# Cross-attention and routed FFN on one core: the tail's steps in another order, and single banks for the last tiles

## What is computed

```python
x = x + attention(layernorm(x), ctx, ctx)        # 16 heads of 16, softmax over 1024 keys, W_O and b_O
n = layernorm(x)
shared = (silu(n @ sw1) * (n @ sw3)) @ sw2       # 256 -> 512 -> 256
s = sigmoid(n @ router_w.T)                      # 8 experts
top2 = top_k(s + router_bias, 2)                 # gates: s of the two, divided by their sum
routed = sum over top2 of gate * (gelu(n @ ew1[e]) @ ew2[e])
out = x + shared + routed
```

## Time and profile before

| | us |
|---|---|
| median of 3 runs | 354.72 |
| lowest, highest | 354.29, 355.25 |
| profiled execution | 355.46 |
| its span | 353.7 |
| TensorE busy in it | 318.8 |
| VectorE, ScalarE, GpSimd busy | 263.1, 220.2, 146.4 |
| mean granted clock of TensorE | 0.973 of full |

### The profile page before, as it was taken

One profiled execution on the slowest core, in us unless ns is written; L12 is line 12 of the kernel. 1 busy time (PEld: TensorE's weight loads), 2 busy tenths in 40 slices (PEclk: granted clock), 3 DMA queues, 4 the chain that ended last, 5 costly groups with the idle time before them and its releaser, 6 DMA issues.

```text
span 353.7 us, 6968 instructions
## 1 busy us (share of the span) xinstructions
PE 318.8 (90%) x2556; PEld 190.0 (54%) x2556; DVE 263.1 (74%) x439; ACT 220.2 (62%) x395; POOL 146.4 (41%) x204
## 2 busy tenths in 40 slices
PE   5787898999999999999999999999999797899970
PEld 2585565333333333333373354344899785799870
DVE  5886998999999999999939941894966735743525
ACT  5562445898989899898928874855134442656410
POOL 6014469104045252566544554375110265335540
PEclk9999999999999999999999995999999899999996
DMA  7679892026061340816349323002401023802635
GB/s 253 276 259 348 288 369 102 0 56 194 5 210 36 108 142 21 260 32 189 120 128 274 98 63 124 6 15 91 135 5 59 32 80 103 281 32 76 213 116 178
DMA packets 29130, 47.54 MB, mean 134 GB/s; under 512 B 6388, under 2 KB 20596, under 8 KB 27412
## 3 DMA queue, kind: packets, MB, share of 16 engines
q1 hardware_dynamic: 27128, 41.70, 37.0%
q0 software_dynamic: 1968, 5.38, 4.2%
HBM read 28.34 MB, written 16.01 MB: 125 GB/s over the span
## 4 chain that ended last, share of the span: by engine, by line
PE 64%; DVE 16%; DMA 6%; ACT 5%; issue 5%; SPq 2%; another core or an unknown queue 1%; POOL 1%; POOLq 0%; ACTq 0%; DVEq 0%
PE psum L1228 20%; PE psum L1415 18%; PE psum L1282 14%; PE psum L1288 8%; DVE negm L1117 4%; DMA PB<-in_ctxT_dram 2%; ACT PB L767 2%; DMA PB<-ys_d 1%; PE psum L1346 1%; PE psum L1325 1%; SPq L435 1%; DMA qs_d<-SWH 1%; ACT TMP L823 1%; DMA EWT<-qs_d 1%
## 5 line engine op out<-in xcount | busy, mean ns | idle before, releaser
L1117 DVE TENSOR_REDUCE negm<-psum 128x1 f32<-128x1024 f32 x128 | 153.7, 1222 | 12.4 <-PE psum L1288 11.9
L767 ACT ACTIVATE PB<-psum 128x512 f32<-128x512 f32 x256 | 138.4, 598 | 32.2 <-PE psum L1282 23.6
L1415 PE MATMUL psum<-PB,VA 128*17 128x256 f32 x1024 | 81.5, 392 | 2.6 <-ACT TMP L823 2.1
L1228 PE MATMUL psum<-EWT,WH 128*128 (+2 forms) x348 | 55.8, 310 | 4.3 <-ACT TMP L802 2.4
L1282 PE MATMUL psum<-EWT 64*128 64x512 f32 x160 | 58.6, 448 | 0.4 <-ACT PB L767 0.3
L1288 PE MATMUL psum<-EWT 64*128 64x512 f32 x160 | 53.5, 450 | 4.4 <-DMA EWT<-qs_d 2.5
L1228 PEld LDWEIGHTS psum<-EWT,WH 128*128 128x128 f32 x348 | 47.3, 195 | 8.5 <-issue 6.8
L1415 PEld LDWEIGHTS psum<-PB,VA 128*17 128x17 f32 x1024 | 17.5, 95 | 46.7 <-issue 35.6
L1282 PEld LDWEIGHTS psum<-EWT 64*128 64x128 f32 x160 | 24.5, 184 | 30.7 <-ACT PB L767 24.1
L1288 PE MATMUL psum<-S 64*128 64x512 f32 x96 | 32.2, 457 | 1.7 <-DVE negm L1117 1.2
L1282 PE MATMUL psum<-S 64*128 64x512 f32 x96 | 33.3, 487 | 0.0
(11 more groups left out here) (219 smaller groups left out, 444.4 us busy)
## 6 DMA issues: line engine op xcount, KB each, us to landing
ks_d<-SWH SPq DMA_DIRECT2D x8, 512.0 KB, 4.4
RAW<-in_ew_dram SPq DMA_DIRECT2D x16, 256.0 KB, 2.9
EWT<-ks_d SPq DMA_DIRECT2D x15, 256.0 KB
EWT<-qs_d SPq DMA_DIRECT2D x30, 128.0 KB
xs_d<-VA SPq DMA_DIRECT2D x1, 3212.5 KB, 16.6
S<-ks_d SPq DMA_DIRECT2D x9, 256.0 KB
S<-qs_d SPq DMA_DIRECT2D x18, 128.0 KB
qs_d<-SWH SPq DMA_DIRECT2D x4, 512.0 KB, 5.3
```

Source lines behind the costliest of these rows:

```text
L767: act.activation(PB[:, n % PR, i * N:(i + 1) * N], bank[t % 3], ACT.Exp, scale=DK ** -0.5).then_inc(exp_done, 1)
L1117: dve.tensor_reduce(negm[:, g % 2, r // QT, r % QT:r % QT + 1], psum[:, k0:k0 + 2, :].rearrange("p a n -> p (a n)"), AX.X, ALU.max, negate ...
L1228: r = pe.matmul(dst, a_hl[u], b_hl[v], start=first and i == 0, stop=last and i == 2)
L1415: last = pe.matmul(acc[32 * j:32 * j + DK + 1, cols], VA[:, b, kp + KP * kk, GH * hg + j, :], PB[:, (4 * q + j) % PR, kk * N:(kk + 1) * N] ...
```

## The change

It gives the steps from the last units on a new order, and with it some operations new places:

- In the stream, `place` part 1 of half 0 moves from five units earlier to behind `norm` 6, `experts` and `gates` of half 0 behind it.
- `tx` and `tt` are divided: VectorE's low parts are steps of their own (`tx_lo`, `tt_lo`).
- `sums` of group 7 goes to bank 3 instead of a ring slot. `oproj_part` of half 1 is in two pieces, groups 0 and 1 ahead of `sums` 7, group 2 behind it. `tx` 0 comes ahead of `oproj`; hidden part 3 (`later[4:]`) behind it.
- `choose` of half 1 comes right behind `router`, with the low parts behind the second `choose`; `ty` 0 comes behind `rank`.
- `gelu_table` is new: a one-element gelu on ScalarE behind the silu of `h` 7 and ahead of the copy of `tx` 4. `gates` of half 1 comes ahead of `h` 4.
- The slots of the tail are named by hand (`tail_slot`), with a `ring_full` for each slot.
- The last three tiles (22, 23, 24) have a bank each (3, 0, 1), an evacuation each and a scatter that waits for its tile alone (`y_pieces`).

```diff
-            todo += [("oproj_part", 0), ("oproj", 0)]
+            todo += [("oproj_part", 0, 0, HG - 1), ("oproj", 0)]
...
-                         (23, ("place", 0, 0)), (23, ("place", 0, 1)), (24, ("experts", 0)), (29, ("gates", 0))):
+                         (23, ("place", 0, 0)), (28, ("place", 0, 1)), (29, ("experts", 0)), (30, ("gates", 0))):
...
-    steps += later[:4] + [("h", 1)] + later[4:] + [("h", 2), ("sums", NG - 1), ("norm", NG - 1), ("oproj_part", 1)]
-    steps += [("h", 3), ("oproj", 1), ("tx", 0), ("y", 0, 0)] + [("stats2", 1, t) for t in range(4)] + [("th", 0)]
-    steps += [("var2", 1), ("tx", 1), ("y", 0, 1), ("y", 0, 2), ("norm2", 1), ("y", 0, 3), ("add_y", 0, 0)]
-    steps += [("add_y", 0, 1), ("xpose2", 1), ("tt", 0), ("th", 1), ("tx", 2), ("exp_table",)]
-    steps += [("logits", 1, t) for t in range(4)] + [("router", 1), ("ty", 0), ("tt", 1), ("choose", 1, 0), ("th", 2)]
-    steps += [("choose", 1, 1), ("tx", 3), ("rank", 1), ("place", 1, 0), ("ty", 1), ("place", 1, 1), ("h_mm", 4)]
-    steps += [("th", 3), ("tt", 2), ("experts", 1), ("h_mm", 5), ("h", 4), ("ty", 2), ("tt", 3), ("h_mm", 6), ("h", 5)]
-    steps += [("h_mm", 7), ("h", 6), ("tx", 4), ("h", 7), ("ty", 3), ("tx", 5), ("th", 4), ("gates", 1)]
+    steps += later[:4] + [("h", 1), ("h", 2), ("oproj_part", 1, 0, 2), ("sums", NG - 1), ("oproj_part", 1, 2, 3)]
+    steps += [("norm", NG - 1), ("tx", 0), ("tx_lo", 0), ("oproj", 1)] + later[4:] + [("stats2", 1, t) for t in range(4)]
+    steps += [("var2", 1), ("h", 3), ("th", 0), ("tx", 1), ("y", 0, 0), ("tt", 0), ("norm2", 1), ("tx_lo", 1)]
+    steps += [("xpose2", 1), ("tt_lo", 0), ("y", 0, 1), ("tx", 2), ("tx_lo", 2), ("add_y", 0, 0), ("exp_table",)]
+    steps += [("logits", 1, t) for t in range(4)] + [("router", 1), ("choose", 1, 0), ("th", 1), ("y", 0, 2), ("tt", 1)]
+    steps += [("choose", 1, 1), ("tt_lo", 1), ("rank", 1), ("place", 1, 0), ("ty", 0), ("place", 1, 1), ("th", 2)]
+    steps += [("tx", 3), ("tx_lo", 3), ("ty", 1), ("y", 0, 3), ("add_y", 0, 1), ("th", 3), ("tt", 2), ("tt_lo", 2)]
+    steps += [("experts", 1), ("gates", 1), ("h_mm", 4), ("h", 4), ("ty", 2), ("tt", 3), ("tt_lo", 3), ("h_mm", 5)]
+    steps += [("h", 5), ("ty", 3), ("h_mm", 6), ("h", 6), ("h_mm", 7), ("h", 7), ("gelu_table",), ("tx", 4), ("tx_lo", 4)]
+    steps += [("tx", 5), ("th", 4), ("tx_lo", 5)]
...
                 steps.append((kind, r))
+                if kind in ("tx", "tt"):
+                    steps.append((kind + "_lo", r))
...
+    tail_slot = {("oproj", 1): 0, ("xpose2", 1): 1, ("y", 0): 0, ("router", 1): 1, ("rank", 1): 1, ("h", 4): 1,
+                 ("h", 5): 0, ("h", 6): 1, ("h", 7): 0, ("y", 1): 1}
+    used = [0, 0]
+    def take(st):
+        slot = len(ring_at) % 2
+        if st in tail_slot:
+            slot = (ring_at[("h", 0)][0] + tail_slot[st]) % 2
+        ring_at[st] = slot, used[slot]
+        used[slot] += 1
...
+        def y_pieces(q):
+            if q < NQ - 2:
+                return [(slice(0, 2 * D), q + 1, bank[3])]
+            return [(slice(j * D, (j + 1) * D), i - 2 * (NQ - 2) + NQ - 1, bank[(3, 0, 1)[i - 2 * (NQ - 2)]][:, 0:D])
+                    for j, i in enumerate(tiles_of(q))]
...
             def scatter_y(q):
-                pool.wait_ge(y_out, q + 1)
                 for j, i in enumerate(tiles_of(q)):
+                    if j < len(y_pieces(q)):
+                        pool.wait_ge(y_out, y_pieces(q)[j][1])
...
                 else:
-                    act.wait_ge(y_done, q + 1)
                     if q >= YR:
                         act.wait_ge(ys_stored[q % YR], ys_count(q - YR))
-                    act.activation(ys[q % YR][:, 0:w], bank[3][:, 0:w], ACT.Copy).then_inc(y_out, 1)
+                    for cols, count, src in y_pieces(q):
+                        act.wait_ge(y_done, count)
+                        act.activation(ys[q % YR][:, cols], src, ACT.Copy).then_inc(y_out, 1)
...
-                elif st[0] == "exp_table":
-                    act.activation(exp_in[:, :], exp_in[:, :], ACT.Exp)
+                elif st[0] in ("exp_table", "gelu_table"):
+                    act.activation(exp_in[:, :], exp_in[:, :], ACT.Exp if st[0] == "exp_table" else ACT.Gelu)
...
+                        dve.wait_ge(last_sums, 1)
+                        dve.tensor_tensor(RC, acc, U[g % 2], ALU.mult).then_inc(sums_read, 1)
...
                     pe.wait_ge(h_lo, q + 1)
-                    if q:
+                    if q == NQ - 1:
+                        pe.wait_ge(gelu_done, NQ)
+                    elif q:
                         pe.wait_ge(y_out, q)
+                    pieces = y_pieces(q)
                     for j, i in enumerate(ts):
+                        if q == NQ - 2 and j:
+                            pe.wait_ge(x_lo, NQ)
+                        dst = pieces[j][2] if len(pieces) > 1 or q == NQ - 1 else bank[3][:, j * D:(j + 1) * D]
...
-                            pe.wait_ge(u_ready, NG)
+                            pe.wait_ge(sums_read, 1)
```

More of the change, by code:

```diff
@@ L322, in xattn_ffn @@
         bias_loaded = [sem(f"bias_loaded{i}") for i in range(2)]
-        ring_full = sem("ring_full")
+        ring_full = [sem(f"ring_full{i}") for i in range(2)]
         ring_empty = [sem(f"ring_empty{i}") for i in range(2)]
@@ L377, in ring_bank, with slot_full, filled @@
         def ring_bank(st, i=0):
-            return bank[4 + 2 * (ring_at[st] % 2) + i]
+            return bank[4 + 2 * ring_at[st][0] + i]
         def slot_empty(st):
-            return ring_empty[ring_at[st] % 2]
+            return ring_empty[ring_at[st][0]]
         def freed(st):
-            return ring_empty[ring_at[st] % 2], ring_at[st] // 2 + 1
+            return slot_empty(st), ring_at[st][1] + 1
+        def slot_full(st):
+            return ring_full[ring_at[st][0]]
+        def filled(st):
+            return slot_full(st), ring_at[st][1] + 1
         def h_bank(p, i):
@@ L478, in sums_in @@
                     done = ("sums", g - 1)
-                    sp.wait_ge(*((scores_done, tile_at[done] + 1) if done in tile_at else (ring_full, ring_at[done] + 1)))
+                    sp.wait_ge(*((scores_done, tile_at[done] + 1) if done in tile_at else filled(done)))
                 for i in range(2):
@@ L829, in _ @@
                     if g == HG:
-                        act.wait_ge(ring_full, ring_at[("oproj", 0)] + 1)
+                        act.wait_ge(*filled(("oproj", 0)))
                     act.activation(ao[g % HG][0], RC, ACT.Copy).then_inc(a_hi, 1)
@@ L1109, in ring_wait @@
             def ring_wait(st):
-                dve.wait_ge(ring_full, ring_at[st] + 1)
+                dve.wait_ge(*filled(st))
             def maxima(m):
@@ L1163, in _ @@
                     g = st[1]
-                    dve.wait_ge(*freed(("sums", g)))
+                    dve.wait_ge(*(freed(("sums", g)) if g < NG - 1 else (sums_read, 1)))
                     bias = bv_sb[:, g % HG:g % HG + 1]
@@ L1422, in _ @@
                         tile_wait(tile_at[st])
-                        o, filled = bank[tile_at[st] % 3], scores_done
-                    else:
-                        ring_wait(st)
-                        o, filled = ring_bank(st), ring_full
+                        o, full = bank[tile_at[st] % 3], scores_done
+                    elif g < NG - 1:
+                        ring_wait(st)
+                        o, full = ring_bank(st), slot_full(st)
+                    else:
+                        pe.wait_ge(u_ready, NG)
+                        o, full = acc, last_sums
                     pe.wait_ge(ru_loaded, 32 * (g + 1))
-                    pe.matmul(o[:, :], selr[:, :], RU[:, :], start=True, stop=True).then_inc(filled, 1)
+                    pe.matmul(o[:, :], selr[:, :], RU[:, :], start=True, stop=True).then_inc(full, 1)
                 elif st[0] in ("oproj_part", "oproj"):
                     b = st[1]
-                    if st[0] == "oproj_part":
-                        groups = range(HG - 1)
+                    groups = range(*st[2:]) if st[0] == "oproj_part" else range(HG - 1, HG)
+                    if groups[0] == 0:
                         pe.wait_ge(pool_split, 1)
                         ring_wait(("oproj", b))
-                    else:
-                        groups = range(HG - 1, HG)
                     pe.wait_ge(a_lo, HG * b + groups[-1] + 1)
```

69 lines of the change are left out of this document (37 added, 32 removed).

## The result

The changed kernel is slower. Side by side, four executions of each, it took 358.61 us in the median (357.05 to 362.08) and the kernel before 354.99 (354.29 to 355.85): ratio 1.015, 95% interval 1.009 to 1.021. The profiled execution took 357.05 us, with a span of 355.3 and a mean granted clock of 0.964. Forecast were 352.4 (350.3 to 355.6).

The account below looks back on a forecast made before the run. TensorE's settled pipeline from about 309 us was unchanged, so its start, held by waits in stream, expert choice and sort, and the end counted. Gains of 0.75 + 1.45 + 0.1 = 2.3 us from 354.72 gave 352.4 us, range 350.3 to 355.6.

Parts of the forecast that it names:

- Part 1: Attention stream: `sums` 6 read near 234, 0.8 us wait gone; `place` part 1 takes 3.0 us, first scatter near 239.4.
- Part 2: Projection: `tx` 0 waits for tiles until 256.0, projection read at 258.15, 0.9 us earlier; logits end 1.8 us earlier.
- rival C: First sort late, `tx` 0 passes delay on; slower, 356.9 us, decided once tiles land after 259.4; chance 0.13.
- Part 3: Expert choice of half 1 before low halves: 4.0 us, `rank` at 276.0, 3.8 earlier; second sort 2.4 earlier.
- Part 4: Behind `h_mm` 7: early table brings about 3.15 us of idle TensorE; pair 7 starts 0.75 us earlier net.
- Rival B: Clock falls in the wait behind `h_mm` 7; `tx` 5 and `th` 4 cost 1.9 us more, 354.3; chance 0.20.
- Part 5: Last tiles: own banks and evacuations let the last scatter start 1.45 us earlier; lower bound 0.
- The sum: Whole kernel: 0.75 + 1.45 us, and 0.1 from shorter evacuations, 2.3 us gained, giving 352.4 us.
- cross-check by idle time: TensorE up to pair 7: 7.1 us idle plus about 1.4 in low clock before, against 8.6 idle in the new order.

Follow-up runs that it names:

- place_back: Changed kernel with `place` part 1, `experts` and `gates` of half 0 back at their old units; 353.89 us, ratio 0.999 to the kernel before.
- end_only: Kernel before with only the last three tiles' own banks, evacuations and scatter waits; 355.35 us against 355.16, ratio 1.002.
- tx0_behind: Changed kernel with `tx` 0 and its low half behind the projection, `place` left late; 355.03 us against 355.16, ratio 0.995.
- fill_first: Changed kernel with 14 unread matmuls in front of `tx` 0 alone; ratio 1.014 to the kernel before.
- again: The changed kernel itself, unaltered, measured and profiled once more; 357.52 us against 355.16, ratio 1.009.
- tile4_first: Changed kernel without the early gelu table, `tx` 4 and its low half ahead of `h` 7; 357.68 us against 354.2, ratio 1.012.
- ty3_behind: Changed kernel without early gelu table, `tx` 4 and its low half ahead of `h` 7, `ty` 3 behind it; 353.85 us, ratio 0.996.
- fill_second: Changed kernel with 14 unread matmuls in front of `tx` 5 alone; ratio 1.012 to the kernel before.
- ty3_tx0: The edits of `ty3_behind` on the changed kernel, with `tx` 0 and its low half behind `oproj` as well; 352.02 us, ratio 0.995.
- both: Changed kernel with the edits of `place_back` and `tile4_first` together; 352.05 us against 354.2, ratio 0.995.
- both_ty3: `both` with `ty` 3 moved behind `h` 7; 349.17 us, ratio 0.988 to the kernel before.

## Why the prediction was wrong

**Part 1, right.** `sums` 6 is read at 233.85 and the wait is gone. From the spreading matmul (233.22) to `evac` 7 it is 11.68 us; in `place_back` and `end_only`, where the stream has its old order, 12.55 and 12.54. That is 0.9 gained, forecast 0.8. The kernel before took 13.54 (from 233.42 in the earlier trace rows), but 1.0 of it is a pause of that one execution behind group 7's last sums, which the forecast carried along unseen. Kernel before, three rows, then the changed kernel:

```profile
244.36 1.49 PE L1415 MATMUL psum<-PB,VA 128*17 128x256 f32 x24
246.63 0.60 ACT L780 ACTIVATE PB<-psum 128x512 f32<-128x512 f32 x1 [0.98 <-remote]
246.96 0.69 DVE L1161 COPY TMP<-psum 128x512 f32<-128x512 f32 x1 [4.63 <-PE psum L1415]
...
243.29 1.49 PE L1452 MATMUL psum<-PB,VA 128*17 128x256 f32 x24
```

From the sums' start to their copy it is 2.60 us there, and 1.61 or 1.62 in all other traces; all three engines start late, and what held them is not shown.

`place` part 1 took 3.0 us, as said, and the first scatter starts at 239.97, forecast 239.4.

**Part 2 is the step that failed.** It had the tiles at 256.0, a wait of 2.4 us and full clock behind it. The load went at 254.45, 2.5 us behind the eighth scatter's end (250.94 + 0.97) where I had taken 1.5 from the other sort; the same sort in the earlier trace rows has 2.6 (247.84 + 0.99 to 251.44), though SyncE was busy with the reciprocals' DMAs there until 251.34. The tiles were used from 257.2 on, 1.2 later than forecast, and TensorE was there at 253.0 instead of 253.6, since the pause of part 1 did not come again. So the wait was 4.15 us. It drew the clock down, for which the sum had nothing: twelve matmuls in 2.57 us where I had 1.6. The read, at 260.27, is 2.1 us behind the forecast's 258.15, 1.2 for the tiles and 1.0 for the clock. From `evac` 7 to the projection's read the forecast was 258.15 - 246.16 = 12.0 us and the trace has 15.4 (the forecast's `evac` 7 stood 1.3 us too late, with the pause); `tx0_behind` and `place_back`, in which the projection does not wait, have 11.1 and 10.6. I had seen the mechanism, as rival C, but let it decide only from 259.4 on, because I counted the tiles' lateness alone and not TensorE's earliness and the clock.

**Part 3, right for an undelayed kernel.** The choice took 278.43 - 274.46 = 3.97 us, forecast 4.0. `rank` came 34.2 us behind `evac` 7, forecast 29.8: 3.4 of the 4.3 are part 2's; beside the rest lies a second piece of low clock (275.1 to 278.5), with no long wait in front of it. The low half of pair 1, costed at nothing, stood ahead of `place` (279.91 + 0.69), which began 0.95 us behind `rank`'s last matmul. `place_back` has `rank` at 28.6. The two scatters in front of the second sort were there as said.

**Part 4: the wait right, its price not.** Idle behind `h_mm` 7 was forecast at 3.15 us and measured at 3.14, with the released engine and the load (1.28, its small activation 1.30 behind its start) as said. Rival B came true with it: the clock fell there, and `tx` 5 and `th` 4 took 1.09 and 2.68 us instead of 0.63 and 1.67, 1.5 more, B's 1.9. The Trainium skill (TensorE: Matmul & The Clock Gate, What's actually happening) says that idleness sends the clock to its lower level; both long waits of this trace (4.15 and 3.14 us) bear that out, and I should have given B more than 0.20. The other rule of the Trainium skill that I weighed (ScalarE: Activation LUTs, What ACT_TABLE_LOAD costs), a drain of 1.38 us on top of the load, is again not in the trace: the activation follows at 304.56.

**Part 5, right in the trace and not in the medians.** From pair 7 to the end 43.7 us were forecast and 42.97 measured; `end_only` has the same gain in its trace and none in its medians.

**The sum.** For `evac` 7 to pair 7 I had 307.7 - 246.16 = 61.5 us. `place_back` has 61.57, the changed kernel 67.4. That `place_back` meets the 61.5 is luck in part: its `rank` is 1.2 us ahead of the forecast's 29.8, and low clock behind `h_mm` 7, for which the sum had nothing, takes that again. What is missing is the late `place` with what hangs on it, 5.9 us in these traces and 3.4 or 5.6 by the ratios. The chances were wrong in taking B and C for alternatives: they came together, one feeding the clock to the other's loss. As written they also add up to 0.60 for faster and 0.15 for slower, where 0.61 and 0.14 stand. The 0.3% that I took as what a measurement can tell was too fine: the interval of the result is 0.6% to either side. And the cross-check by idle time balanced idle against idle, with no term for the clock that the new waits cost.

## What to carry over

In an in-order queue, a step that waits for a DMA belongs behind the work that others wait for: moving `tx` 0 by one place was worth 3.7 us of trace, though its data came no earlier. When a reordering gives TensorE a new wait like those of 3.1 and 4.2 us here, price the wait twice, once as idle time and once as clock behind it, and look for a product that can be put into it before looking for a way to shorten it (`ty` 3, moved there, with `place` back, turned a loss of 1% into a gain of 1.2%). Keep the rest of such a change only where an experiment with that part alone shows it.

## What the runs showed of the hardware

- **A saved stretch of low clock can come back elsewhere.** `fill_first` traded the 3.4 us behind the wait for the first tiles for twice as much at the logits. In all six traces that keep the late `place` with `tx` 0 at the head and are not filled twice (changed, again, `tile4_first`, `ty3_behind`, `fill_first`, `fill_second`), the clock is low for 10.2 us between `evac` 7 and pair 7, in different places. Where it falls differs between kernels that execute the same instructions there: at the logits not in `place_back`, `tx0_behind` and `ty3_tx0`, but in `both` (low from 269.1 for 6.8 us) and `both_ty3` (from 267.5 for 6.8); not in the kernel before, but in `end_only` (from 271.9 for 6.8), whose `rank` comes 1.9 us later. What decides it was not tried.
- **The eighth of a row of indirect DMAs is late in every sort**, by 2.12 us here (250.94), 2.40 and 2.80 in the earlier trace rows, and by 2.06 to 2.45 in all others; the five scatters at the end follow one another without it.
- **Executions of the same kernel spread over 6 to 8 us** in the larger sets (350.4 to 356.9 for the kernel before, 354.2 to 362.5 for the changed one), and five rounds still leave an interval of 1% between two such kernels. Stretches of a trace, counted from a common event, told the larger differences apart when the medians did not (the changed kernel agreed with itself within 0.3 us); for differences under two microseconds they are no better, as `end_only` shows.
